# A two-layer attention kernel: steps between the score products reordered, four elementwise pieces moved from VectorE to GpSimd and ScalarE

## The chip, the cores and the metric

The kernel runs on one core of one Trainium2 chip. The metric is the device time of one execution in microseconds (us), lower is better. The engines are called as the profile calls them: PE is TensorE, DVE is VectorE, ACT is ScalarE, POOL is GpSimd, SP is the engine that issues most transfers. Each engine works through its own instructions in order and waits on semaphores.

## The reference

The input x has 128 sequences of 64 tokens of 256 features. Two layers follow one another.

```
L0:  x_mod = rms(x) * (1 + scale_msa) + shift_msa
     q, k, v = split(x_mod @ qkv_w);  q, k = rope(rms(q) * w), rope(rms(k) * w)
     x = x + gate_msa * (softmax(q k^T / 4) v @ proj_w + proj_b)
     h = rms(x) * (1 + scale_mlp) + shift_mlp
     x = x + gate_mlp * ((silu(h @ w1) * (h @ w3)) @ w2)
L1:  self_feat = concat(x, cond or 0 where the row sum is 0) @ W_self^T + b_self
     for d in 0, 1:                        # the adjacency and its transpose
         A = adjacency (64 x 64 x 11), first 20 columns
         aff = q k^T / 4, -9e15 where sum(A) == 0, plus A @ w_bias + b_bias
         output += softmax(aff) @ kv, through Wout, + bout
     result = x + relu(self_feat + output)
```

Shift and scale come per sequence from a condition vector. The float32 products are made of reduced-precision parts: each operand is split into a high part and a low rest (`nh`, `nl` and others).

## The kernel before

Features lie on the partitions, tokens in the free dimension. The 8192 tokens are done in NM = 32 blocks of MT = 256 tokens (4 sequences), so a typical tile is 128x512 (DC = 2 halves of the features by 256 tokens). `ORDER` is a schedule written out by hand: for each engine a list of (a, step, n), run once per iteration m; an entry stands for the step of block m + a. So an iteration works on up to four blocks at once: the second layer of block m, the MLP of block m + 1, the first attention of m + 2, and norm and qkv of m + 3. An iteration is called a period below. Engines meet only through semaphores, called signals here; `wait(engine, signal, m, n)` waits for the n-th count of block m, and `wait_last` for everything of the blocks before m, which protects a buffer. `wait_free` on PE waits until the last readers of a PSUM bank are done.

The steps that matter below, with the lines of the profile:

- End of an iteration. PE makes the MLP's last products (`mlp_down`, L744 is its last part). Its input is a product on DVE, which ACT copies to `gh` (L982), and whose rest POOL makes as `gl` (L1372). DVE adds the second attention to `sf` (`mix1`, L1333), takes an inverse root (`rope_scale`, L1190), and makes the result `out` (L1339): y = max(sf, 0) + x2. SP stores y (L507).
- Start of the next iteration. DVE scales q and k (`rope`, L1196, once for each of two token tiles), then gates the MLP's output (`mlp_down`, L1262), POOL adds the residual x1 (L1420), ACT copies to `nh` (L995), POOL makes the rest `nl` (L1372). PE sums the rows with `ones_r` and multiplies with the self weights (`self`). DVE's `mlp_down` waits for `relu_done` of the block before, because `out` reads x2.
- POOL goes on with `heads` (`kbd`, L1384), adds x_res to x1 (`proj`, L1415) and splits sf (`self_split`, L1372).
- DVE reduces the weighted edges and makes their bias (`edge_masks`, L1284, L1285, L1287). PE makes the scores of the first attention, and DVE takes their maximum and subtracts it (`score_max` L1206, `score` L1211, for two tiles), with `norm1_squares` (L1140), `norm1_mean` (L1145) and `k1` (L1294) in between.
- The norm of the MLP: ACT squares x1, DVE adds the two halves (L1140), PE takes the mean (`norm1_mean`, L580), DVE adds eps, POOL takes the power (L1368), PE spreads the result over the partitions (`norm1_apply`, L587), POOL scales (L1404), DVE multiplies (L1153) and shifts (L1162), ACT copies to `nh` and POOL makes `nl`. The norm of the next block (`norm0_...`, scale L1394) does the same for qkv.

```
            def out(m, n):
                wait(dve, summed1, m, DC)
                wait_last(dve, out_s, m)
                nc.vector.scalar_tensor_tensor(y[:, :, :], sf[:, :, :], 0.0, x2[:, :, :], ALU.max, ALU.add)
            def mlp_down(m, n):
                wait(dve, down_done, m, 1)
                wait_last(dve, relu_done, m)
```

Of the kernel before, what the change touches and what calls it, by code (L numbers as in the profile page):

```python
# [37 lines left out]
DC = D // P  # L38
# [33 lines left out]
LOW_PARTS = {("norm0_shift", 0): (2, 4), ("rope", 1): (4, 7), ("score", 1): (7, 9), ("mix", 1): (9, 12), ("mlp_up", 1): (12, 14)}  # L72
# [13 lines left out]
        (0, "q1", 0), (0, "q1", 1), (0, "q1_low", 0), (1, "norm1_mean", 0), (0, "q1_low", 1), (1, "norm1_apply", 0),  # L86
# [7 lines left out]
        (2, "rope", 0), (2, "rope", 1), (0, "mlp_down", 0), (1, "mixT", 0), (1, "proj", 0), (0, "row_mask", 0),  # L94
        (0, "edge_masks", 0), (2, "score_max", 0), (2, "score", 0), (1, "norm1_squares", 0), (2, "score_max", 1),
# [5 lines left out]
        (3, "rope_scale", 0), (0, "out", 0),  # L101
    ],
    "Activation": [
        (2, "rope_scale", 0), (0, "mlp_split", 2), (1, "mixT", 0), (0, "x2_split", 0),
# [73 lines left out]
def build_program(nc, d):  # L178
    with ExitStack() as ctx:
# [3 lines left out]
        def signal(name, per=1):  # L183
            return Signal(ctx.enter_context(nc.semaphore(name)), per)
# [197 lines left out]
        edge_masked, edge_ready = signal("edge_masked"), signal("edge_ready")  # L382
# [5 lines left out]
        relu_done = signal("relu_done")  # L388
# [40 lines left out]
        def _(sp):  # L429
# [444 lines left out]
        def _(act):  # L874
# [122 lines left out]
            def self_feat(m, n):  # L997
                if isinstance(m, int) and m == 0:
                    act.wait_ge(weight_lo.sem, len(PIECES))
                wait(act, self_ps, m, 1)  # L1000
                wait_last(act, relu_done, m)
# [24 lines left out]

            def score1(m, t):
                wait(act, shifted1, m, t + 1)
                e_v = e1[t][:, :, :, 0:NKV].rearrange("p h a k -> p (h a) k")
                nc.scalar.activation(e_v, e_v, ACT.Exp).then_inc(exps1.sem, 1)  # L1030

            def probs_t1(m, t):
# [10 lines left out]
                "score1": score1, "probsT1": probs_t1, "edges": edges,  # L1043
# [6 lines left out]
        def by_seq(ap):  # L1050
            return ap.rearrange("p c (b s) -> p c b s", s=S)

        @block.vector
        def _(dve):
# [66 lines left out]
            def rotation_tables():  # L1121
                dve.wait_ge(sines.sem, 1)
                half = DH // 2
                for i in range(2):
                    for a in range(2):
                        nc.vector.tensor_tensor(cosw[:, i, a * half:(a + 1) * half], lnw[:, i, a * half:(a + 1) * half],
                                                ang[:, 1, :], ALU.mult)
                        last = nc.vector.scalar_tensor_tensor(sinw[:, i, a * half:(a + 1) * half], ang[:, 0, :],
                                                              (1.0, -1.0)[a], lnw[:, i, a * half:(a + 1) * half],
                                                              ALU.mult, ALU.mult)  # L1130
                last.then_inc(table_step.sem, 1)
                dve.wait_ge(table_step.sem, 9)
                low_parts(*LOW_PARTS["norm0_shift", 0])

            dve.wait_ge(zeros_set.sem, 6)
            dve.wait_ge(biases_set.sem, 2)

            def norm1_squares(m, n):
                wait(dve, squares[1], m, 1)
                nc.vector.tensor_tensor(x1_sq[:, 0, :], x1_sq[:, 0, :], x1_sq[:, 1, :], ALU.add).then_inc(square_sums.sem, 1)  # L1140
# [195 lines left out]
            def out(m, n):  # L1336
                wait(dve, summed1, m, DC)
                wait_last(dve, out_s, m)
                nc.vector.scalar_tensor_tensor(y[:, :, :], sf[:, :, :], 0.0, x2[:, :, :], ALU.max, ALU.add)\  # L1339
                    .then_inc(relu_done.sem, 1)  # L1340

            run_steps(dve, "DVE", {
                "norm1_squares": norm1_squares, "norm1_mean": norm1_mean, "norm1_apply": norm_apply(1), "qkv": qkv, "rope_scale": rope_scale,
                "rope": rope, "score_max": score_max, "score": score, "norm0_apply": norm_apply(0),
                "norm0_shift": norm_shift(0), "norm1_shift": norm_shift(1), "mix": mix, "mixT": mix_t, "proj": proj,
                "mlp_up": mlp_up, "mlp_down": mlp_down, "row_mask": row_mask, "edges": edges,
                "k1": k1, "score1_bias": score1_bias, "score1_max": score1_max, "score1": score1, "soft1_inverse": soft1_inverse,
                "edge_masks": edge_masks, "soft1": soft1, "mix1": mix1, "out": out,
            }, {step: partial(low_parts, *pieces) for step, pieces in LOW_PARTS.items()}
                | {("norm0_shift", 0): rotation_tables, ("rope", 1): cond_split})  # L1350
# [3 lines left out]
        def _(pool):  # L1354
# [83 lines left out]
            def soft1(m, t):  # L1438
# [7 lines left out]
                "x2_split": x2_split, "self_split": self_split, "soft1": soft1, "norm0_scale": norm0_scale, "norm1_scale": norm1_scale, "edges": edges,  # L1446
            })
# [47 lines left out]
```

## Time and profile before

| | before |
|---|---|
| median of 3 runs | 1367.35 us (1363.63 to 1369.65) |
| the profiled execution | 1372.13 us, its span 1370.3 us |
| PE busy | 1296.1 us, 95% |
| DVE busy | 1190.3 us, 87% |
| ACT busy | 861.6 us, 63% |
| POOL busy | 718.7 us, 52% |
| granted PE clock | 0.976 of full speed |
| DMA | 53 GB/s mean |

The span is the time between the first and the last instruction that the profiler saw. The busy times overlap. The kernel repeats one pattern, so one period in the middle can be read in place of the whole: its timeline gives for each engine the start of an instruction, its duration, the line, the tiles, and in brackets how long the engine sat idle before it and who ended the wait.

### The profile page before, as it was taken

To read this page: it belongs to the slowest core of one execution; us is meant where nothing else is said; L and a number is where in the kernel's file an instruction comes from. 1 tells how busy PE (TensorE), PEld (TensorE's weight loads), DVE (VectorE), ACT (ScalarE), POOL (GpSimd) and SP (SyncE) were. 2 spreads that over 40 slices of the span, in tenths; PEclk is the share of its full clock that TensorE was granted. 3 is DMA by queue.
4 is the path that set the end of the run, shared out by engine and by line. 5 is a ranking of instruction groups with operands and counts; after the bars stand their busy time and mean duration, and the time that the engine had idled before them with its cause. 6 is when DMAs were issued, how large, how long until landed. Compare 5 with 4: busy or idle time off the path is not lost. (4 is left out here: it accounts for less than half of the span.)

```text
span 1370.3 us, 50527 instructions
## 1 busy us (share of the span) xinstructions
PE 1296.1 (95%) x19956; PEld 1178.2 (86%) x19956; DVE 1190.3 (87%) x2067; ACT 861.6 (63%) x1722; POOL 718.7 (52%) x676
## 2 busy tenths in 40 slices
PE   5689999999999999999999999999999999999985
PEld 4578888988888898888889888888988898999874
DVE  7569899989889898989999898999999999989763
ACT  5456666667666666666666676666667666666542
POOL 2136555555655555565555456555545655554551
PEclk9689999999999999999999999999999999999996
DMA  6101111101111110111111111111111111111110
GB/s 218 60 24 47 61 60 44 59 31 44 59 59 57 46 59 31 44 59 60 54 50 55 35 44 59 59 52 52 47 44 44 59 59 52 52 39 45 45 40 24
DMA packets 72164, 72.98 MB, mean 53 GB/s; under 512 B 5952, under 2 KB 65728, under 8 KB 72128
## 3 DMA queue, kind: packets, MB, share of 16 engines
q1 hardware_dynamic: 71840, 71.96, 16.2%
q10 hardware_dynamic: 288, 0.52, 0.1%
q8 instruction: 25, 0.41, 0.1%
q14 instruction: 11, 0.09, 0.0%
HBM read 55.42 MB, written 17.04 MB: 53 GB/s over the span
## 5 line engine op out<-in xcount | busy, mean ns | idle before, releaser
L1372 POOL TENSOR_TENSOR gl<-gf,gh 128x512 fp32r<-128x512 f32 x96 | 124.7, 1299 | 222.5 <-ACT gh L982 222.5
L519 PE MATMUL psum<-nh,w_lo 128*128 128x256 f32 x704 | 181.0, 289 | 0.0
L519 PE MATMUL psum<-nh,w_hi 128*128 128x256 f32 x704 | 175.4, 281 | 0.0
L1441 POOL TENSOR_TENSOR e<-e,inv 128x640 f32<-128x640 f32 x64 | 82.2, 1284 | 138.6 <-DVE inv L1328 138.6
L1372 POOL TENSOR_TENSOR nl<-xn,nh 128x512 fp32r<-128x512 f32 x64 | 96.0, 1500 | 91.4 <-ACT nh L920 91.4
L519 PEld LDWEIGHTS psum<-nh,w_lo 128*128 128x128 f32 x704 | 133.3, 189 | 0.3 <-issue 0.2
L519 PEld LDWEIGHTS psum<-nh,w_hi 128*128 128x128 f32 x704 | 133.4, 190 | 0.0
L519 PE MATMUL psum<-nl,w_hi 128*128 128x256 f32 x704 | 114.8, 281 | 0.0
L982 ACT ACTIVATE gh<-gf 128x512 fp32r<-128x512 f32 x96 | 60.3, 628 | 61.3 <-DVE gf L1256 60.6
L519 PEld LDWEIGHTS psum<-nl,w_hi 128*128 128x128 f32 x704 | 97.2, 189 | 0.2 <-POOL nl L1372 0.2
L519 PE MATMUL psum<-qkv_lo,nh 128*128 128x512 f32 (+1 forms) x256 | 88.4, 356 | 8.2 <-ACT nh L920 7.4
L967 ACT ACTIVATE aoh<-psum 128x512 fp32r<-128x512 f32 x32 | 19.1, 598 | 109.5 <-PE psum L679 109.5
L519 PE MATMUL psum<-gh,w_lo 128*128 128x256 f32 x320 | 81.6, 289 | 1.6 <-ACT gh L982 0.8
L519 PE MATMUL psum<-qkv_hi,nh 128*128 128x512 f32 (+1 forms) x256 | 82.2, 343 | 0.0
L670 PEld LDWEIGHTS psum<-vb,pT 128*64 128x64 f32 x2048 | 67.1, 141 | 17.5 <-issue 12.7
L1420 POOL TENSOR_TENSOR x<-x 128x256 f32<-128x256 f32 x64 | 45.7, 735 | 69.2 <-DVE x L1262 69.2
L1384 POOL TENSOR_TENSOR kbd<-qkT,consts 128x512 f32<-128x512 f32 x64 | 66.5, 1060 | 29.3 <-ACT qkT L948 29.3
L1206 DVE TENSOR_REDUCE mx<-psum 128x16 f32<-128x1024 f32 x64 | 77.8, 1215 | 2.3 <-PE psum L635 2.2
L1211 DVE TENSOR_TENSOR e<-psum,mx 128x1024 f32<-128x1024 f32 x64 | 78.1, 1220 | 1.4
L519 PE MATMUL psum<-gh,w_hi 128*128 128x256 f32 x320 | 78.1, 278 | 0.0
L655 PE MATMUL psum<-consts,e 128*128 128x128 f32 x512 | 73.3, 289 | 4.4 <-ACT e L953 4.3
L1256 DVE TENSOR_TENSOR gf<-gf,psum 128x512 f32<-128x512 f32 x96 | 66.0, 688 | 11.4 <-PE psum L519 0.3
(193 smaller groups left out, 4319.1 us busy)
## 6 DMA issues: line engine op xcount, KB each, us to landing
adj<-in_adj SPq DMA_DIRECT2D x32, 440.0 KB, 3.3
x_in<-in_x SPq DMA_DIRECT2D x32, 256.0 KB, 2.7
xn<-in_xT SPq DMA_DIRECT2D x32, 256.0 KB, 3.7
x_res<-in_xT SPq DMA_DIRECT2D x32, 256.0 KB, 3.7
v_rows<-stage SPq DMA_DIRECT2D x32, 256.0 KB, 2.0
vb<-v_rows SPq DMA_DIRECT2D x128, 64.0 KB, 1.9
out_T<-y SPq DMA_DIRECT2D x32, 256.0 KB, 2.1
stage<-in_qkv SPq DMA_DIRECT2D x2, 384.0 KB, 6.2
```

Of the source, the lines that this page charges most:

```text
L519: last = nc.tensor.matmul(out, lhsT, rhs, start=start and i == 0, stop=stop and i == len(terms) - 1)
L655: last = nc.tensor.transpose(pT_out[t][j // 4][:, j % 4, :], e0[t][:, 2 * pair(j):2 * pair(j) + 2, :].rearrange("p h s -> p (h s)"), ident ...
L670: last = nc.tensor.matmul(mix_ps[t][s * S:(s + 1) * S, j, :], pT0[:, j, s * S:(s + 1) * S], vb[:, t, s, j, :], start=True, stop=True, tile ...
L967: nc.scalar.activation(aoh[:, :, :].rearrange("p c t -> p (c t)"), aoT_ps, ACT.Copy).then_inc(mixed_hi.sem, 1)
L982: nc.scalar.activation(gh[:, 2 * n:2 * n + 2, :], gf[:, :, :], ACT.Copy).then_inc(g_hi.sem, 1)
L1206: nc.vector.tensor_reduce(mx0_v, s_v[t], AX.X, ALU.max).then_inc(maxima.sem, 1)
L1211: nc.vector.tensor_tensor(e0_v[t], s_v[t], mx0_v.unsqueeze(3).to_broadcast([P, NG, 4, S]), ALU.subtract).then_inc(shifted_s.sem, 1)
L1256: nc.vector.tensor_tensor(gf[:, :, :], gf[:, :, :], u_ps[n], ALU.mult).then_inc(g_done.sem, 1)
L1372: return nc.gpsimd.tensor_tensor(out, full, hi.bitcast(F32), ALU.subtract)
L1384: nc.gpsimd.tensor_tensor(kbd[:, t, :, :, :, :].rearrange("p c s h k -> p (c s) h k"), qkT[t][:, 1, :, :].rearrange("p c (s k) -> p (c s) ...
L1420: nc.gpsimd.tensor_tensor(x2[:, o, :], x2[:, o, :], x1[:, o, :], ALU.add).then_inc(x2_done.sem, 1)
L1441: nc.gpsimd.tensor_tensor(e_v, e_v, inv1[t][:, :].unsqueeze(2).to_broadcast([P, ND * H, NKV]), ALU.mult)\
```

## The change

Work is moved between engines, and steps within an engine's list.

1. `out`: ACT makes y = relu(sf) (new signal `relu_kept`), and POOL adds x2 to y (`relu_done`), after its `mlp_up` 2 and before its `mlp_down`. DVE's instruction goes. `self` on ACT waits for `relu_kept` in place of `relu_done`. ACT's `rope_scale` and `mlp_split` 2 move from the head of the list to its end, one block further on, so that their place in time order is the same.
2. `norm1_squares` moves from DVE to POOL, behind `self_split`. On PE `norm1_mean` moves ahead of `q1_low` 0; on DVE `k1` moves ahead of `norm1_mean`, and both ahead of the second `score_max`.
3. `norm0_shift` moves from DVE to POOL, ahead of `norm0_apply`.
4. The edges: the reduction (`edge_values`) moves ahead of `proj` on DVE. The sum with the bias becomes two additions on POOL (`edge_sum`, new signal `edge_offset`), between `norm0_scale` and `norm1_apply`. SP's load of the next edges waits for `edge_count` and `edge_float` of the block before, no longer for `edge_masked`.
5. The parts of the weights that were split behind `norm0_shift` in the first block are split behind `norm0_apply`.

```diff
 "PE":
-  (0, "q1", 1), (0, "q1_low", 0), (1, "norm1_mean", 0), (0, "q1_low", 1), (1, "norm1_apply", 0),
+  (0, "q1", 1), (1, "norm1_mean", 0), (0, "q1_low", 0), (0, "q1_low", 1), (1, "norm1_apply", 0),
 "DVE":
-  (1, "mixT", 0), (1, "proj", 0), (0, "row_mask", 0),
-  (0, "edge_masks", 0), (2, "score_max", 0), (2, "score", 0), (1, "norm1_squares", 0), (2, "score_max", 1),
-  (1, "norm1_mean", 0), (0, "k1", 0), (2, "score", 1), (1, "norm1_apply", 0), (1, "norm1_shift", 0),
-  (3, "norm0_apply", 0), (3, "norm0_shift", 0), (0, "score1_bias", 0),
+  (1, "mixT", 0), (0, "edge_values", 0), (1, "proj", 0),
+  (0, "row_mask", 0), (0, "edge_masks", 0), (2, "score_max", 0), (2, "score", 0), (0, "k1", 0),
+  (1, "norm1_mean", 0), (2, "score_max", 1), (2, "score", 1), (1, "norm1_apply", 0), (1, "norm1_shift", 0),
+  (3, "norm0_apply", 0), (0, "score1_bias", 0),
...
-  (3, "rope_scale", 0), (0, "out", 0),
+  (3, "rope_scale", 0),
 "Activation":
-  (2, "rope_scale", 0), (0, "mlp_split", 2), (1, "mixT", 0),
+  (1, "mixT", 0),
...
+  (3, "rope_scale", 0), (1, "mlp_split", 2), (0, "out", 0),
 "Pool":
-  (1, "proj", 0), (0, "self_split", 0), (3, "norm0_mean", 0), (1, "norm1_mean", 0), (1, "norm1_scale", 0),
-  (3, "norm0_scale", 0), (1, "norm1_apply", 0), (3, "norm0_apply", 0), (0, "soft1", 0), (1, "mlp_up", 0),
-  (0, "soft1", 1), (1, "edges", 0), (1, "mlp_up", 1), (1, "mlp_up", 2), (1, "mlp_down", 0), (1, "x2_split", 0),
+  (1, "proj", 0), (0, "self_split", 0), (1, "norm1_squares", 0), (3, "norm0_mean", 0), (1, "norm1_mean", 0), (1, "norm1_scale", 0),
+  (3, "norm0_scale", 0), (0, "edge_sum", 0), (1, "norm1_apply", 0), (3, "norm0_shift", 0), (3, "norm0_apply", 0), (0, "soft1", 0), (1, "mlp_up", 0),
+  (0, "soft1", 1), (1, "edges", 0), (1, "mlp_up", 1), (1, "mlp_up", 2), (0, "out", 0), (1, "mlp_down", 0), (1, "x2_split", 0),
...
-                wait_last(sp, edge_masked, m)
+                wait_last(sp, edge_count, m)
+                wait_last(sp, edge_float, m)
...
+            def out(m, n):                      # ACT
+                wait(act, summed1, m, DC)
+                wait_last(act, out_s, m)
+                nc.scalar.activation(y[:, :, :], sf[:, :, :], ACT.Relu).then_inc(relu_kept.sem, 1)
...
+            def out(m, n):                      # POOL
+                wait(pool, relu_kept, m, 1)
+                nc.gpsimd.tensor_tensor(y[:, :, :], y[:, :, :], x2[:, :, :], ALU.add).then_inc(relu_done.sem, 1)
...
+            def norm1_squares(m, n):
+                wait(pool, squares[1], m, 1)
+                nc.gpsimd.tensor_tensor(x1_sq[:, 0, :], x1_sq[:, 0, :], x1_sq[:, 1, :], ALU.add).then_inc(square_sums.sem, 1)
...
+            def edge_sum(m, n):
+                wait(pool, edge_value, m, 1)
+                nc.gpsimd.tensor_tensor(edge_v[:, :, :], edge_v[:, :, :],
+                                        all_edges(edge_b[:, :]), ALU.add).then_inc(edge_offset.sem, 1)
+                wait(pool, edge_masked, m, 1)
+                wait(pool, edge_offset, m, 1)
+                wait_last(pool, biased1, m)
+                nc.gpsimd.tensor_tensor(edge_bias[:, :, :], edge_v[:, :, :], edge_n[:, :, :], ALU.add).then_inc(edge_ready.sem, 1)
...
+            def norm0_shift(m, n):
+                wait(pool, normed[0], m, 1)
+                nc.gpsimd.tensor_tensor(by_seq(xn[0][:, :, :]), by_seq(xn[0][:, :, :]),
+                                        per_seq(mods[:, SHIFT_A:SHIFT_A + DC, bass.ds(m * MB, MB)]), ALU.add)\
+                    .then_inc(shifted[0].sem, 1)
```

## Rows read from the trace of the kernel before

**Rows 1.** Windows view of one period: busy time and instructions of each engine.

```profile
701.10:741.20 40.10, 39.54 (x625) 35.95 (x624) 36.52 (x64) 26.39 (x54) 22.39 (x21) 1.00 0.16 51
```

**Rows 2.** Timeline of PE: start us, duration us, engine, line, operation, tiles, count.

```profile
703.88 0.27 PE L744 MATMUL psum<-gl,w_hi 64*128 64x256 f32 x1
...
707.06 0.40 PE L519 MATMUL psum<-nh,ones_r 128*128 128x256 f32 x2
...
707.77 0.49 PE L519 MATMUL psum<-nl,ones_r 128*128 128x256 f32 x2
...
713.94 0.64 PE L519 MATMUL psum<-sf_lo,q_hi 128*128 128x256 f32 x4
...
714.42 0.50 PE L580 MATMUL psum<-consts,x_sq 128*128 128x1 f32 x4
...
715.94 0.43 PE L587 MATMUL psum<-consts,rms_inv 128*128 128x128 f32 x2 [0.44 <-POOL rms_inv L1368]
...
717.78 1.50 PE L830 MATMUL psum<-kbd,q1T 32*64 32x40 f32 x128
...
728.47 0.39 PE L519 MATMUL psum<-qkv_lo,nh 128*128 128x512 f32 x1
```

**Rows 3.** Timeline of DVE in the same period.

```profile
701.72 1.53 DVE L1339 SCALAR_TENSOR_TENSOR y<-sf,x 128x512 f32<-128x512 f32 x1
703.17 1.28 DVE L1196 TENSOR_TENSOR qr<-qr,qk_inv 128x512 f32<-128x512 f32 x2
704.38 0.74 DVE L1262 TENSOR_TENSOR x<-psum,mods 128x256 f32<-128x256 f32 x2
...
707.48 0.88 DVE L1237 SCALAR_TENSOR_TENSOR x<-psum,consts,mods 128x256 f32<-128x256 f32 x2 [1.30 <-PE psum L519]
...
708.64 1.05 DVE L1284 TENSOR_REDUCE edge_v<-q1T 128x80 f32<-128x880 f32 x1
...
709.83 1.21 DVE L1287 SCALAR_TENSOR_TENSOR edge_bias<-edge_v,consts,edge_n 128x80 f32<-128x80 f32 x1
...
710.96 1.21 DVE L1206 TENSOR_REDUCE mx<-psum 128x16 f32<-128x1024 f32 x1
...
713.35 0.41 DVE L1140 TENSOR_TENSOR x_sq<-x_sq 128x256 f32<-128x256 f32 x1
...
714.96 0.16 DVE L1145 TENSOR_SCALAR rms_root<-psum 128x2 f32<-128x2 f32 x1
...
716.21 1.21 DVE L1211 TENSOR_TENSOR e<-psum,mx 128x1024 f32<-128x1024 f32 x1
...
719.60 0.69 DVE L1162 TENSOR_TENSOR xn<-xn,mods 128x512 f32<-128x512 f32 x1
```

**Rows 4.** Timeline of POOL in the same period.

```profile
701.41 1.29 POOL L1372 TENSOR_TENSOR gl<-gf,gh 128x512 fp32r<-128x512 f32 x1 [5.62 <-ACT gh L982]
...
704.87 1.42 POOL L1420 TENSOR_TENSOR x<-x 128x256 f32<-128x256 f32 x2 [2.17 <-DVE x L1262]
...
706.26 1.44 POOL L1372 TENSOR_TENSOR nl<-x,nh 128x256 fp32r<-128x256 f32 x2
...
709.67 1.27 POOL L1415 TENSOR_TENSOR x<-x,x_res 128x512 f32<-128x512 f32 x1
...
711.25 1.29 POOL L1372 TENSOR_TENSOR sf_lo<-sf,sf_hi 128x512 fp32r<-128x512 f32 x1 [0.31 <-ACT sf_hi L1009]
...
715.20 0.69 POOL L1368 TENSOR_TENSOR rms_inv<-rms_root,minus_half 128x2 f32<-128x2 f32 x1 [1.57 <-DVE rms_root L1145]
...
716.85 1.05 POOL L1394 TENSOR_TENSOR xn<-xn,mods 128x512 f32<-128x512 f32 x1
719.67 1.76 POOL L1372 TENSOR_TENSOR nl<-xn,nh 128x512 fp32r<-128x512 f32 x1 [1.78 <-ACT nh L920]
```

**Rows 5.** Timeline of ACT in the same period.

```profile
706.33 0.42 ACT L995 ACTIVATE nh<-x 128x256 fp32r<-128x256 f32 x1 [0.27 <-POOL x L1420]
```

**Rows 6.** Instructions that write y: shortest, median and longest in ns.

```profile
L1339 DVE SCALAR_TENSOR_TENSOR y<-sf,x x32: 692/1540/1761, 140.4 to 1367.1; 128x512 f32<-128x512 f32 x32
```

More of the change, by code:

```diff
@@ L71 @@
 HIGH_PARTS = {("norm0_apply", 0): (2, 5), ("heads", 1): (5, 9), ("probsT", 0): (9, 12), ("mlp_split", 0): (12, 14)}
-LOW_PARTS = {("norm0_shift", 0): (2, 4), ("rope", 1): (4, 7), ("score", 1): (7, 9), ("mix", 1): (9, 12), ("mlp_up", 1): (12, 14)}
+LOW_PARTS = {("norm0_apply", 0): (2, 4), ("rope", 1): (4, 7), ("score", 1): (7, 9), ("mix", 1): (9, 12), ("mlp_up", 1): (12, 14)}
 BANK = {
@@ L85 @@
         (2, "heads", 1), (1, "proj", 0), (0, "self", 0), (0, "self_cond", 0), (2, "score", 0), (0, "k1", 0),
-        (0, "q1", 0), (0, "q1", 1), (0, "q1_low", 0), (1, "norm1_mean", 0), (0, "q1_low", 1), (1, "norm1_apply", 0),
+        (0, "q1", 0), (0, "q1", 1), (1, "norm1_mean", 0), (0, "q1_low", 0), (0, "q1_low", 1), (1, "norm1_apply", 0),
         (2, "probsT", 0),
@@ L93 @@
     "DVE": [
-        (2, "rope", 0), (2, "rope", 1), (0, "mlp_down", 0), (1, "mixT", 0), (1, "proj", 0), (0, "row_mask", 0),
-        (0, "edge_masks", 0), (2, "score_max", 0), (2, "score", 0), (1, "norm1_squares", 0), (2, "score_max", 1),
[2 rows of a table removed]
+        (2, "rope", 0), (2, "rope", 1), (0, "mlp_down", 0), (1, "mixT", 0), (0, "edge_values", 0), (1, "proj", 0),
+        (0, "row_mask", 0), (0, "edge_masks", 0), (2, "score_max", 0), (2, "score", 0), (0, "k1", 0),
[2 rows of a table added]
         (0, "score1_bias", 1), (0, "score1", 0), (2, "mix", 0), (0, "score1_max", 1), (0, "soft1", 0),
@@ L387, in build_program @@
         mixed1, summed1 = signal("mixed1", TILES), signal("summed1", DC)
-        relu_done = signal("relu_done")
+        relu_kept, relu_done = signal("relu_kept"), signal("relu_done")
         cond_rows_s = signal("cond_rows_s", 16)
@@ L1000, in self_feat @@
                 wait(act, self_ps, m, 1)
-                wait_last(act, relu_done, m)
+                wait_last(act, relu_kept, m)
                 for o in range(DC):
@@ L1042, in _ @@
                 "mlp_up": mlp_up, "mlp_split": mlp_split, "x2_split": x2_split, "self": self_feat, "self_split": self_split, "q1": q1, "v1": v1,
-                "score1": score1, "probsT1": probs_t1, "edges": edges,
+                "score1": score1, "probsT1": probs_t1, "edges": edges, "out": out,
             }, {("norm0_mean", 0): first_weights, ("rope_scale", 0): gate_and_mlp_mods} | {step: partial(high_parts, *pieces) for step, pieces in HIGH_PARTS.items()})
@@ L1132, in rotation_tables @@
                 dve.wait_ge(table_step.sem, 9)
-                low_parts(*LOW_PARTS["norm0_shift", 0])
+                low_parts(*LOW_PARTS["norm0_apply", 0])
             dve.wait_ge(zeros_set.sem, 6)
             dve.wait_ge(biases_set.sem, 2)
-            def norm1_squares(m, n):
-                wait(dve, squares[1], m, 1)
-                nc.vector.tensor_tensor(x1_sq[:, 0, :], x1_sq[:, 0, :], x1_sq[:, 1, :], ALU.add).then_inc(square_sums.sem, 1)
             def norm1_mean(m, n):
@@ L1277, in edges, with edge_values @@
                 wait(dve, adj_s, m, 16)
+                wait_last(dve, edge_ready, m)
                 nc.vector.tensor_reduce(flat[0], adj[:, :, :, :].rearrange("p t e l -> p (t e) l"), AX.X, ALU.add)\
                     .then_inc(edge_count.sem, 1)
+            def edge_values(m, n):
+                wait(dve, edge_weighted, m, 1)
+                wait_last(dve, edge_ready, m)
+                nc.vector.tensor_reduce(flat[1], adw, AX.X, ALU.add).then_inc(edge_value.sem, 1)
             def edge_masks(m, n):
-                wait(dve, edge_weighted, m, 1)
                 wait(dve, edge_count, m, 1)
-                nc.vector.tensor_reduce(flat[1], adw, AX.X, ALU.add).then_inc(edge_value.sem, 1)
                 nc.vector.tensor_scalar(flat[0], flat[0], 0.0, NEG, ALU.is_le, ALU.mult).then_inc(edge_masked.sem, 1)
-                wait(dve, edge_masked, m, 1)
-                nc.vector.scalar_tensor_tensor(flat[2], flat[1], edge_b[:, :], flat[0], ALU.add, ALU.add)\
-                    .then_inc(edge_ready.sem, 1)
             def k1(m, n):
@@ L1334, in mix1 @@
                                                    ALU.add, ALU.add).then_inc(summed1.sem, 1)
[L1336 to L1340, printed above, removed]
             run_steps(dve, "DVE", {
-                "norm1_squares": norm1_squares, "norm1_mean": norm1_mean, "norm1_apply": norm_apply(1), "qkv": qkv, "rope_scale": rope_scale,
+                "norm1_mean": norm1_mean, "norm1_apply": norm_apply(1), "qkv": qkv, "rope_scale": rope_scale,
                 "rope": rope, "score_max": score_max, "score": score, "norm0_apply": norm_apply(0),
-                "norm0_shift": norm_shift(0), "norm1_shift": norm_shift(1), "mix": mix, "mixT": mix_t, "proj": proj,
+                "norm1_shift": norm_shift(1), "mix": mix, "mixT": mix_t, "proj": proj,
                 "mlp_up": mlp_up, "mlp_down": mlp_down, "row_mask": row_mask, "edges": edges,
                 "k1": k1, "score1_bias": score1_bias, "score1_max": score1_max, "score1": score1, "soft1_inverse": soft1_inverse,
-                "edge_masks": edge_masks, "soft1": soft1, "mix1": mix1, "out": out,
+                "edge_masks": edge_masks, "edge_values": edge_values, "soft1": soft1, "mix1": mix1,
             }, {step: partial(low_parts, *pieces) for step, pieces in LOW_PARTS.items()}
-                | {("norm0_shift", 0): rotation_tables, ("rope", 1): cond_split})
+                | {("norm0_apply", 0): rotation_tables, ("rope", 1): cond_split})
         @block.gpsimd
@@ L1446, in _ @@
                 "x2_split": x2_split, "self_split": self_split, "soft1": soft1, "norm0_scale": norm0_scale, "norm1_scale": norm1_scale, "edges": edges,
+                "norm1_squares": norm1_squares, "edge_sum": edge_sum, "norm0_shift": norm0_shift, "out": out,
             })
```

6 lines of the change are left out of this document (4 added, 2 removed), and 2 rows, old and new, of the table ORDER.

## The prediction

> **What bounds the kernel.** I read the windows view of one period first, then the timelines of PE, DVE, POOL and ACT over that period, and last the durations of the instruction that goes. A period is 40.10 us. PE is busy 39.54 of it, DVE 36.52, ACT 26.39, POOL 22.39 [rows 1]. The reader is to see that PE is the tightest engine, with 0.56 us a period that the profile calls idle, and that DVE, though busy nine tenths, is second. So work taken off DVE pays only where PE waits for DVE, and work put on POOL costs where PE waits for POOL. Two places are like that.
>
> Place A is the turn of the period. The MLP's last product starts on PE at 703.88 and ends at 704.15 [rows 2]. DVE then gates it at 704.38, just as `rope` ends (703.17 + 1.28 = 704.45) [rows 3]; POOL adds it at 704.87 and makes its rest until 707.70 (706.26 + 1.44) [rows 4]; ACT's second copy ends at 706.75 [rows 5]. PE starts the row sums at 707.06, 0.31 us behind that copy, and their low part at 707.77, 0.07 us behind POOL [rows 2, 4]. So a delay of the gate reaches PE whole. POOL does not rest from 704.87 to 710.94 (709.67 + 1.27) [rows 4], hence neither can it catch up there.
>
> Place B is the MLP's norm. PE takes the mean at 714.42, DVE adds eps at 714.96, POOL's power ends at 715.89 and PE goes on at 715.94 after the wait in brackets, 0.44 us [rows 2, 3, 4]. That wait is most of the idle PE time.
>
> **The change at place A: POOL adds x2.** DVE's y instruction took 1.53 us, from 701.72 to 703.25 [rows 3]. Its shortest is 692 ns, its median 1540 [rows 6]. POOL's `gl` ran from 701.41 to 702.70 [rows 4], so y ended 0.55 us behind it: an instruction with both inputs in SBUF stood still until POOL was through. The same is seen at L1287, a small 128x80 sum that took 1.21 us and ended at 711.04, 0.10 us behind POOL's addition at 710.94 [rows 3, 4]. So the two exclude each other for a whole instruction. That sets the sum. The next DVE instruction, `rope`, also has both inputs in SBUF, and takes y's slot: it will stand still from 701.72 to 702.70. Relu on ACT is ready in time: a 128x256 ACT instruction takes 0.42 [rows 5], so 128x512 takes at most 0.84, and from 701.72, when the sum for `out` is surely done, it ends by 702.56. Then three pieces share the time from 702.70, one after another: rope 0, rope 1 and POOL's addition. Before, it was y's rest 0.55 and 1.28 less an overlap of 0.08, which brought the end of rope to 704.45. After, it is 0.55 for the first rope, 1.27 for the addition (L1415 has its form and size [rows 4]) and about 0.60 for the second rope: 705.12. In each of the three possible orders the sum is the same, and the gate needs both rope and the addition (`relu_done`). It starts 0.07 before the end, as before: 705.10 if rounded up, against 704.38. The loss is **0.72 us** a period. Behind the gate on DVE wait the low part of `mixT` and `proj`'s gate, which has 1.30 us of idle time before it [rows 3]; on POOL all of 704.87 to 710.94. Behind ACT's Relu and its wait is the first copy of the next period, whose input comes from PE after 704.15, so that wait costs nothing.
>
> [...]
>
> The bounds of this loss: 0 if rope does not contend; 0.46 if the 0.31 of slack before the row sums, less 0.05 for PE's reaction (715.89 to 715.94), can be used and the low part does not bind; 0.72 + 0.31 = 1.03 if the heads' transposes wait for the second rope as well. I take 0.72, since the low part had 0.07 to spare only.
>
> No row shows a Relu. If it brought a table load, the add could start later than 702.70, but both ropes would pass first, and the end stays near 705.1: nothing is added to the sum.
>
> [...]
>
> **The change at place B.** `norm1_squares` on DVE was 0.41 us [rows 3]. POOL is free behind `sf_lo` at 712.54 (711.25 + 1.29) and needs 0.71 for a 128x256 addition (1.42 for two [rows 4]), so it is done at 713.25. PE takes the mean in place of the four low products at 713.94 [rows 2], and DVE may add eps 0.54 later (714.96 - 714.42), at 714.48. DVE has by then `k1`: the first maximum and subtraction still end at 713.35 (slot of L1140), and k1 with the eps instruction takes 716.21 - 714.96 = 1.25 us [rows 3]. So the root is out at about 714.68, POOL's power runs 714.76 to 715.45, and PE goes on at 715.50. Before it was 715.94: a gain of **0.44 us**. The same low products are still done before it, by about 715.3. The second subtraction starts 0.33 earlier (L1140's share without overlap) and ends at 716.21 - 0.33 + 1.21 = 717.09; PE's second-layer scores, at 717.78 before, can start at 717.34. So that gain holds. Bounds: 0 if POOL's queue is late, 0.56 at most, all of PE's idle time.
>
> **What is hidden.** `norm0_shift`: 0.69 on DVE [rows 3], about 1.05 on POOL (L1394, the same broadcast form [rows 4]). It comes behind `nl` of the other norm (719.67 + 1.76) and its rest is made by about 724; PE's qkv reads it at 728.47 [rows 2]. Without those 4 us of cover it would cost 1.05 - 0.69 = 0.36 a period. `edge_sum`: the trace shows no such POOL instruction; it lies between nothing and 0.71 each (128x256), so at most 1.42 together, in the 1.78 us that POOL idled before 719.67 [rows 4]. I take 0.37 each, between the ends since 128x80 is nearer to the small one. The 1.05 us reduction L1284 moves into the 1.30 us of idle before L1237 [rows 3]; L1287 goes. But the next DVE instruction, the first maximum, then waits for PE's scores, so of the 2.26 us that leave this place at most 0.1 shows, which I leave out. SP: the store waits about 1.3 to 1.9 us longer, and behind it the condition rows and three loads. They are read 4 us or more later. The next edges are loaded earlier and read late in the period. The moved split of the weights concerns the first block alone: nothing.
>
> **Sum.** DVE loses 3.8 us of work a period, its waits for POOL counted in (1.53, 1.21, 0.69, 0.41), POOL gains about 3.8, yet PE's path gets 0.72 - 0.44 = +0.28 us. Of 32 blocks some 30 turn with all four blocks at work: +8.4 us. At the very end, relu and the addition stand bare: 0.62 (estimated from 0.42 for half the size) + 1.27 - 0.69 = +1.2. Together +9.6. The profiled execution took 1372.13 (span 1370.3), and would take 1381.7. It lies 4.8 above the median of the runs, 1367.35, so for that I say 1377.0, +0.7%.
>
> **Rivals.** *The addition is hidden*: POOL idles 2.17 us before 704.87 [rows 4], more than 1.27. If rope does not have to take turns with it, the gate can start 0.1 behind PE's end, at 704.25, and the gain of place B stays: -0.57 x 30 + 1.2 = -16, 1351.5. For it: rope's second input is only 64 columns, broadcast. Against it: L1287's were small too and it waited. It decides if rope's two instructions end before POOL's addition or run beside it at 0.68 each. *Loss alone*: POOL's longer queue eats the gain of place B: 0.72 x 30 + 1.2 = +22.8, 1390. Against it: POOL has 0.69 us to spare before 713.94. *DVE was the bound*: 3.8 us a period, -114; the 39.54 of PE exclude more than 0.56 x 30 = -17, so it gives 1351 with the first. *Slack hides a part*: 0.46 - 0.44, about 0 a period, 1369, no change to be measured.
>
> **Numbers.** The forecast 0.50, hidden addition or DVE as the bound together 0.27, slack 0.13, loss alone 0.10. A measurement of this kernel can tell about 0.5%, 6.8 us. Of the forecast's 0.50 a fifth stays within that. So slower 0.40 + 0.10 = 0.50, same 0.10 + 0.13 = 0.23, faster 0.27. The range takes in both outer cases: 1350 to 1391. The likeliest case's own range is 1370 to 1386 (a loss between 0.5 and 1.0 a period less the gain).
>
> **What would show it.** In the profile after: a period of 40.4 us; the first or the second rope instruction of each pair near 1.5 us or more in place of 0.68; the gate at least 0.6 us later behind PE's last MLP product than now (0.50 from start to start); a new PE wait before the low row sums, for POOL's `nl`; the wait before PE's `norm1_apply` nearly gone. I am wrong if rope stays at 0.68, or if the gate follows PE's end at once.

## The result and the profile after

The changed kernel takes 1374.19 us (median of 19 runs, 1370.12 to 1376.6), the kernel before 1368.48 us (median of 19 runs, 1363.48 to 1373.65). The ratio on record is 1.0033, with a 95% interval of 1.0022 to 1.0044. By it the change makes the kernel 4.5 us slower (3.0 to 6.0); the two medians differ by 5.7 us. Either is less than the 0.5% that the forecast counts as a change. I had forecast +9.6 us.

The windows view of one period of the changed kernel, from one gate (`mlp_down` on DVE, now L1265) to the next; the columns are those of [rows 1].

```profile
703.20:743.39 40.19, 39.94 (x624) 36.05 (x623) 34.87 (x61) 26.92 (x55) 26.32 (x26) 1.00 0.15 51
```

The period is 40.19 us in place of 40.10. DVE is busy 34.87 in place of 36.52, POOL 26.32 in place of 22.39. PE is busy 39.94 in place of 39.54, though it does the same products: some are shown longer, as the two high row sums below, 0.50 in place of 0.40 [rows 2]. So "busy" of PE is no measure of what can be gained here: an experiment below makes the same products in a whole period of 39.71 us, less than the 39.94 that PE is called busy here.

The turn of the period. DVE's timeline of the changed kernel, which answers to rows of [rows 3]:

```profile
700.16 3.12 DVE L1199 TENSOR_TENSOR qr<-qr,qk_inv 128x512 f32<-128x512 f32 x2
703.20 0.74 DVE L1265 TENSOR_TENSOR x<-psum,mods 128x256 f32<-128x256 f32 x2
...
709.71 1.23 DVE L1209 TENSOR_REDUCE mx<-psum 128x16 f32<-128x1024 f32 x1 [2.07 <-PE psum L637]
...
713.30 0.16 DVE L1148 TENSOR_SCALAR rms_root<-psum 128x2 f32<-128x2 f32 x1
...
714.63 1.23 DVE L1214 TENSOR_TENSOR e<-psum,mx 128x1024 f32<-128x1024 f32 x1
```

ACT's Relu in the same period:

```profile
699.70 0.64 ACT L1032 ACTIVATE y<-sf 128x512 f32<-128x512 f32 x1
```

POOL's timeline, which answers to [rows 4]:

```profile
699.75 1.30 POOL L1370 TENSOR_TENSOR gl<-gf,gh 128x512 fp32r<-128x512 f32 x1 [5.64 <-ACT gh L984]
701.00 1.73 POOL L1422 TENSOR_TENSOR y<-y,x 128x512 f32<-128x512 f32 x1
703.69 1.43 POOL L1418 TENSOR_TENSOR x<-x 128x256 f32<-128x256 f32 x2 [0.96 <-DVE x L1265]
705.09 1.42 POOL L1370 TENSOR_TENSOR nl<-x,nh 128x256 fp32r<-128x256 f32 x2
...
713.53 0.69 POOL L1366 TENSOR_TENSOR rms_inv<-rms_root,minus_half 128x2 f32<-128x2 f32 x1 [0.55 <-DVE rms_root L1148]
...
716.19 0.32 POOL L1439 TENSOR_TENSOR edge_v<-edge_v,consts 128x80 f32<-128x80 f32 x1
716.74 0.76 POOL L1444 TENSOR_TENSOR edge_bias<-edge_v,edge_n 128x80 f32<-128x80 f32 x1 [0.23 <-POOL edge_v L1439]
...
719.31 1.04 POOL L1448 TENSOR_TENSOR xn<-xn,mods 128x512 f32<-128x512 f32 x1
```

The reader is to see the three pieces in turn. The two rope instructions take 3.12 us in place of 1.28. A timeline over a narrower window parts them:

```profile
700.16 1.43 DVE L1199 TENSOR_TENSOR qr<-qr,qk_inv 128x512 f32<-128x512 f32 x1
...
701.51 1.76 DVE L1199 TENSOR_TENSOR qr<-qr,qk_inv 128x512 f32<-128x512 f32 x1
```

The first stands still behind `gl` (until 701.05) and ends at 701.59. The addition stands still behind the first rope (it takes 1.73; at the end of the run, alone, 1.26) and ends at 702.73. The second rope stands still behind the addition and ends at 703.28 (700.16 + 3.12). From `gl`'s end to the gate it is 703.20 - 701.05 = 2.15 us, and was 704.38 - 702.70 = 1.68 [rows 3, 4]: 0.47 us later.

PE's timeline, which answers to [rows 2]:

```profile
702.22 0.27 PE L746 MATMUL psum<-gl,w_hi 64*128 64x256 f32 x1
...
705.62 0.50 PE L521 MATMUL psum<-nh,ones_r 128*128 128x256 f32 x2
706.56 0.51 PE L521 MATMUL psum<-nl,ones_r 128*128 128x256 f32 x2
...
708.37 1.21 PE L637 MATMUL psum<-kbd,qkT 32*64 32x128 f32 x64
...
712.76 0.50 PE L582 MATMUL psum<-consts,x_sq 128*128 128x1 f32 x4
...
714.28 0.43 PE L589 MATMUL psum<-consts,rms_inv 128*128 128x128 f32 x2
...
716.22 1.50 PE L832 MATMUL psum<-kbd,q1T 32*64 32x40 f32 x128
```

Counted from the start of `gl`, the low row sums stand at 706.56 - 699.75 = 6.81 us, and stood at 707.77 - 701.41 = 6.36: +0.45, and +0.47 one product on. The second layer's scores (L832) stand at 16.47 and stood at 16.37: +0.10. So PE loses 0.47 at place A and gets 0.38 back at place B (0.39 by the periods of the experiments), and the period grows by 0.09 us. The wait in brackets before L589 is gone.

Over 29 periods that is 2.6 us. At the end of the run, ACT's Relu starts at 1367.08 and the addition ends at 1367.78 + 1.26 = 1369.04; before, y ended at 1367.1 + 0.69 = 1367.8 [rows 6]: +1.2. Together 3.8 us, inside the measured 3.0 to 6.0.

### The profile page after: what moved, and what is told of

It reads as the page before. It is cut to its first block and busy times, and to the rows that moved or that the text cites. A ratio compares the mean times of both kernels' runs of the same rounds, so it can differ in the third digit from the quotient of the medians.

```text
span 1371.6 us, 50740 instructions
## 1 busy us (share of the span) xinstructions
PE 1304.2 (95%) x19956; PEld 1176.5 (86%) x19956; DVE 1141.2 (83%) x1939; ACT 878.0 (64%) x1754; POOL 843.4 (61%) x836
## 5 line engine op out<-in xcount | busy, mean ns | idle before, releaser
L1370 POOL TENSOR_TENSOR nl<-xn,nh 128x512 fp32r<-128x512 f32 x64 | 83.1, 1298 | 48.2 <-ACT nh L922 48.2
L1199 DVE TENSOR_TENSOR qr<-qr,qk_inv 128x512 f32<-128x512 f32 x64 | 95.3, 1528 | 1.4
L1042 ACT ACTIVATE pT<-psum 128x512 f32<-128x512 f32 x64 | 38.3, 598 | 59.1 <-PE psum L849 58.4
L849 PE MATMUL psum<-consts,e 128*128 128x128 f32 x512 | 69.9, 280 | 5.9 <-POOL e L1465 5.9
```

The source lines that it names most:

```text
L849: last = nc.tensor.transpose(pT1_out[t][j // 4][:, j % 4, :], e1[t][:, 2 * pair(j):2 * pair(j) + 2, :, :].rearrange("p h a k -> p (h a k)" ...
L1042: nc.scalar.activation(pT1[:, 0:4, :], pT1_out[t][0], ACT.Copy).then_inc(pT1_a.sem, 1)
L1199: nc.vector.tensor_tensor(q_v, q_v, qk_inv[:, t, :].unsqueeze(2).to_broadcast([P, 2 * H, DH]), ALU.mult)\
L1370: return nc.gpsimd.tensor_tensor(out, full, hi.bitcast(F32), ALU.subtract)
```

## The experiments

All times are against the kernel before on the same chip. The experiments ran on three chips, so ratios and periods are compared, not times. The period is read from gate to gate.

**Place A alone.** The kernel before, with `out` moved as in the change and nothing else.

```diff
 # the kernel before
-  "DVE": (0, "out", 0)   y = max(sf, 0) + x2
+  "Activation": (0, "out", 0)   y = relu(sf)
+  "Pool": (1, "mlp_up", 2), (0, "out", 0), (1, "mlp_down", 0)   y = y + x2
```

> The kernel before, with out alone moved (Relu on ACT, the addition of x2 on POOL). Theory: at the turn of the period the two rope instructions and the addition take turns, and PE gets 0.48 us a period later to the low row sums, as in the changed kernel (from gl's end to the gate 2.15 us in place of 1.68). With nothing to give it back the period is 40.10 + 0.48 = 40.58 us, and the time about 14 + 1.5 us longer than before, +1.1%. Rival one, the loss comes from the longer POOL queue around the norm (squares, edge sum, shift): this kernel is then within 0.2% of before. Rival two, ACT's and POOL's hops are hidden by PE's slack: the same, no change.

It took 1382.85 us, ratio 1.0105 (1.0085 to 1.0126). The timeline of DVE in this kernel, two gates:

```profile
706.74 0.74 DVE L1268 TENSOR_TENSOR x<-psum,mods 128x256 f32<-128x256 f32 x2
...
747.35 0.74 DVE L1268 TENSOR_TENSOR x<-psum,mods 128x256 f32<-128x256 f32 x2
```

The period is 40.61 us, +0.51. Both rivals fall: the moved result alone costs 14 us (12 to 17).

**Place A undone.** The changed kernel, with `out` back on DVE.

```diff
 # the changed kernel
-  "Activation": (0, "out", 0)   "Pool": (0, "out", 0)
+  "DVE": (3, "rope_scale", 0), (0, "out", 0)   y = max(sf, 0) + x2
```

> The changed kernel, with out back on DVE as one instruction. Theory: the turn costs nothing again and the gain at the norm stays: 40.19 - 0.48 = 39.71 us a period, about 0.39 x 29 = 11 us under before, -0.8%. Rival: the loss is in the other moves; then it stays at 40.1 to 40.2 us a period, +0.1 to +0.3% against before.

It took 1358.66 us, ratio 0.9924 (0.9903 to 0.9944).

```profile
738.11 0.74 DVE L1260 TENSOR_TENSOR x<-psum,mods 128x256 f32<-128x256 f32 x2
...
777.82 0.74 DVE L1260 TENSOR_TENSOR x<-psum,mods 128x256 f32<-128x256 f32 x2
```

The period is 39.71 us, to the hundredth as expected. So the change holds a gain of 0.39 us a period and spends 0.48 of it on the moved result.

**The size of the addition.** Two kernels change it and leave Relu and the order as they are. In the first, POOL adds two columns only, so x2 is missing in the rest of the result.

```diff
 # the changed kernel
-  nc.gpsimd.tensor_tensor(y[:, :, :], y[:, :, :], x2[:, :, :], ALU.add).then_inc(relu_done.sem, 1)
+  nc.gpsimd.tensor_tensor(y[:, 0, 0:2], y[:, 0, 0:2], x2[:, 0, 0:2], ALU.add).then_inc(relu_done.sem, 1)
```

> The changed kernel with POOL's addition cut to two columns of one half; the rest of x2 is not added to the result. Relu on ACT, the signals and their order stay. Theory one, the time of the shared turn (rope, addition, rope) makes the loss: gate again 2.85 to 2.97 us behind gl's start, 39.6 to 39.75 us a period, -0.8% against before. Theory two, the hops through ACT and POOL (Relu, two signals, POOL's own start) make it: it stays within 0.15 of 40.19 us.

It took 1358.16 us, ratio 0.9925 (0.9899 to 0.9950). POOL's timeline and DVE's gates:

```profile
731.70 0.64 POOL L1422 TENSOR_TENSOR y<-y,x 128x2 f32<-128x2 f32 x1
```

```profile
733.36 0.76 DVE L1265 TENSOR_TENSOR x<-psum,mods 128x256 f32<-128x256 f32 x2 [0.47 <-PE psum L746]
...
773.06 0.76 DVE L1265 TENSOR_TENSOR x<-psum,mods 128x256 f32<-128x256 f32 x2 [0.47 <-PE psum L746]
```

The period is 39.70 us. The gate now waits for PE, and starts 2.92 us behind `gl`'s start (730.44), as before the change (2.97). So the hops through ACT and POOL cost nothing, and the time in the shared turn does. The small addition took 0.64 us, where its shortest in this run is 0.19: it too stood behind the first rope.

In the second kernel the addition is made twice, with one more signal between the two, so the result has x2 twice.

```diff
 # the changed kernel
+  nc.gpsimd.tensor_tensor(y[:, :, :], y[:, :, :], x2[:, :, :], ALU.add).then_inc(once.sem, 1)
+  wait(pool, once, m, 1)
   nc.gpsimd.tensor_tensor(y[:, :, :], y[:, :, :], x2[:, :, :], ALU.add).then_inc(relu_done.sem, 1)
```

> The changed kernel with the addition of x2 done twice by POOL; the result has x2 twice. Theory: another 1.27 us in the chain to the gate, plus some 0.1 us for the signal between, all of it on PE's path: 41.5 us a period, +38 us against the changed kernel. If only the semaphore order mattered and POOL's idle time could take the addition, it would stay under 40.6.

It took 1419.24 us, ratio 1.0375 (1.0348 to 1.0403).

```profile
720.76 1.73 POOL L1422 TENSOR_TENSOR y<-y,x 128x512 f32<-128x512 f32 x1
722.56 1.60 POOL L1424 TENSOR_TENSOR y<-y,x 128x512 f32<-128x512 f32 x1
```

```profile
724.40 0.76 DVE L1265 TENSOR_TENSOR x<-psum,mods 128x256 f32<-128x256 f32 x2 [1.37 <-POOL y L1424]
...
766.03 0.76 DVE L1265 TENSOR_TENSOR x<-psum,mods 128x256 f32<-128x256 f32 x2 [1.37 <-POOL y L1424]
```

The period is 41.63 us, +1.44. The second rope slipped in between the two additions: the second addition took 1.60 in place of 1.26, though it had started only 0.07 behind the first one's end. The gate starts 4.90 us behind the start of `gl` (719.50), and started 3.45 behind it in the changed kernel (703.20 - 699.75). So the whole delay of the gate reaches PE, to 0.01 us.

**The gate between the ropes.**

```diff
 # the changed kernel
 "DVE":
-  (2, "rope", 0), (2, "rope", 1), (0, "mlp_down", 0),
+  (2, "rope", 0), (0, "mlp_down", 0), (2, "rope", 1),
 "PE":
-  (2, "heads", 1), (1, "proj", 0), (0, "self", 0),
+  (1, "proj", 0), (2, "heads", 1), (0, "self", 0),
```

> The changed kernel, with DVE's gate (mlp_down 0) between the two rope instructions and PE's heads 1 behind proj. Theory: rope and the addition exclude each other, but the gate reads PSUM and only waits for the addition's end; it starts some 0.1 us behind the addition, 1.75 us behind gl's end in place of 2.15. PE then has no transposes to fill its wait for aoh, so some of it is given back: the low row sums come about 0.2 us earlier, 40.0 us a period, about 0.0% against before. Rival, the gate is late because of what comes before the addition (Relu, gl): then it starts where it started, and the period is 40.2 us or more.

It took 1385.84 us, ratio 1.0126 (1.0104 to 1.0148): a miss. DVE's timeline, then POOL's:

```profile
712.59 1.43 DVE L1199 TENSOR_TENSOR qr<-qr,qk_inv 128x512 f32<-128x512 f32 x1
715.40 0.76 DVE L1265 TENSOR_TENSOR x<-psum,mods 128x256 f32<-128x256 f32 x2 [1.38 <-POOL y L1422]
716.07 1.10 DVE L1199 TENSOR_TENSOR qr<-qr,qk_inv 128x512 f32<-128x512 f32 x1
717.10 0.68 DVE L1229 TENSOR_TENSOR aol<-psum,aoh 128x512 fp32r<-128x512 f32 x1
```

```profile
713.43 1.73 POOL L1422 TENSOR_TENSOR y<-y,x 128x512 f32<-128x512 f32 x1
715.91 1.87 POOL L1418 TENSOR_TENSOR x<-x 128x256 f32<-128x256 f32 x2 [0.74 <-DVE x L1265]
```

The gate did start earlier, 1.93 us behind `gl`'s end in place of 2.15, but 0.24 behind the addition where I expected 0.1. Then the second rope met POOL's next piece, the addition of x1: rope took 1.10 in place of 0.68, POOL 1.87 in place of 1.43, and both `aol` (PE waited 0.3 us for it) and `nl` came later. PE also had no transposes to fill its wait for `aoh` (0.41 us). The period is 40.64 us. The turn was moved, not removed. The number fits the rival (40.2 or more), but its reason does not: the gate did not start where it had started.

**Place B, the order of q1.**

```diff
 # the changed kernel, "PE"
-  (0, "q1", 0), (0, "q1", 1), (1, "norm1_mean", 0), (0, "q1_low", 0), (0, "q1_low", 1),
+  (0, "q1", 0), (0, "q1_low", 0), (0, "q1", 1), (1, "norm1_mean", 0), (0, "q1_low", 1),
```

> The changed kernel, with PE's order q1 0, q1_low 0, q1 1, norm1_mean, q1_low 1, so that ACT can copy q1's first half sooner. Theory: in the changed kernel PE waits 0.2 us before norm0_apply for ACT's copy out of the same PSUM bank, because both q1_low stand behind norm1_mean; here the wait goes and the period is 40.0 us, -0.2 us x 29 = -6 us against the changed kernel, so -0.1% against before. Rival: that wait is the issue of the many semaphore waits on PE; then nothing changes, 40.19 us, +0.3%.

It took 1390.35 us, ratio 1.0151 (1.0129 to 1.0173), the period is 40.67 us: a miss, by a slip of mine. With `q1_low` 0 ahead, the mean stands 0.47 us later on PE behind the first attention's scores (L637 at 718.02, L582 at 722.88; 708.37 and 712.76 in the changed kernel). DVE's next steps all wait behind the eps instruction. DVE's timeline, then PE's:

```profile
721.75 1.25 DVE L1298 SCALAR_TENSOR_TENSOR kbd<-psum,consts 128x160 f32<-128x160 f32 x4
723.41 0.16 DVE L1148 TENSOR_SCALAR rms_root<-psum 128x2 f32<-128x2 f32 x1 [0.41 <-PE psum L582]
723.50 1.23 DVE L1209 TENSOR_REDUCE mx<-psum 128x16 f32<-128x1024 f32 x1
724.75 1.23 DVE L1214 TENSOR_TENSOR e<-psum,mx 128x1024 f32<-128x1024 f32 x1
```

```profile
724.40 0.43 PE L589 MATMUL psum<-consts,rms_inv 128*128 128x128 f32 x2 [0.44 <-POOL rms_inv L1366]
...
726.34 0.89 PE L832 MATMUL psum<-kbd,q1T 32*64 32x40 f32 x68 [0.42 <-DVE e L1214]
```

The slip is worth having. It splits the two things that end at place B: PE's last wait is not for the norm but for `e`, the second subtraction, and L832 follows its end (725.98) by 0.36 us. In the kernel's text PE's `score1` waits for `shifted_s`, this subtraction's signal, because both layers' scores use the same PSUM bank. The distance is the same before (717.42 to 717.78 [rows 2, 3]) and after (715.86 to 716.22), so already before the change it was `e` that PE's second-layer scores waited for.

**Place B, squares or norm.** On top of the kernel with `out` back, the squares go back to DVE, and PE's order stays.

```diff
 # the changed kernel with out back on DVE
-  "Pool": (0, "self_split", 0), (1, "norm1_squares", 0), (3, "norm0_mean", 0),
+  "Pool": (0, "self_split", 0), (3, "norm0_mean", 0),
-  "DVE": (2, "score_max", 0), (2, "score", 0), (0, "k1", 0),
+  "DVE": (2, "score_max", 0), (2, "score", 0), (1, "norm1_squares", 0), (0, "k1", 0),
```

> The kernel of the run before with out back on DVE (39.72 us a period), and norm1_squares back on DVE as well, behind the first subtraction and ahead of k1; PE's mean stays early. Theory one, the chain at place B is DVE's own queue: from the scores two maxima, two subtractions, k1 and the eps instruction stand one behind another up to PE's second-layer scores, so the 0.33 us of the squares come back whole: 40.05 us a period, -0.1% against before. Theory two, as predicted, the chain is the norm's (mean, power, PE's wait for it): DVE's squares would be done by the time PE takes the mean, so the period stays at 39.7, -0.8%.

It took 1365.74 us, ratio 0.9978 (0.9961 to 0.9995); the gates stand at 702.34 and 742.34, a period of 40.00 us. DVE's timeline, then PE's:

```profile
748.86 1.22 DVE L1208 TENSOR_REDUCE mx<-psum 128x16 f32<-128x1024 f32 x1 [2.07 <-PE psum L637]
750.11 1.22 DVE L1213 TENSOR_TENSOR e<-psum,mx 128x1024 f32<-128x1024 f32 x1
751.25 0.41 DVE L1142 TENSOR_TENSOR x_sq<-x_sq 128x256 f32<-128x256 f32 x1
751.59 1.25 DVE L1297 SCALAR_TENSOR_TENSOR kbd<-psum,consts 128x160 f32<-128x160 f32 x4
752.76 0.15 DVE L1147 TENSOR_SCALAR rms_root<-psum 128x2 f32<-128x2 f32 x1
752.82 1.22 DVE L1208 TENSOR_REDUCE mx<-psum 128x16 f32<-128x1024 f32 x1
754.07 1.22 DVE L1213 TENSOR_TENSOR e<-psum,mx 128x1024 f32<-128x1024 f32 x1
```

```profile
755.65 1.50 PE L832 MATMUL psum<-kbd,q1T 32*64 32x40 f32 x128 [0.40 <-DVE e L1213]
```

Of the 0.39 us, 0.29 are gone with the squares on DVE, though the mean was ready in time: PE began it at 751.91, and DVE added eps 0.85 us later, where 0.54 is enough (712.76 to 713.30 in the changed kernel). So at place B DVE's own queue is what pays, from the first maximum to the end of the second subtraction. It takes 717.42 - 710.96 = 6.46 us before, 715.86 - 709.71 = 6.15 in the changed kernel and 755.29 - 748.86 = 6.43 here.

Most of the last tenth comes from in front of that queue. PE's scores of the first attention in the kernel before:

```profile
709.56 1.21 PE L635 MATMUL psum<-kbd,qkT 32*64 32x128 f32 x64
```

The first maximum started 710.96 - 709.56 = 1.40 us behind them, right behind the sum of the edges, and starts 709.71 - 708.37 = 1.34 behind them in the changed kernel, and as much here. But the queue is not alone. In the changed kernel DVE adds eps 0.54 us behind PE's mean, as before (714.42 to 714.96 [rows 2, 3]), just as `k1` ends (712.11 + 1.25 = 713.36): mean and queue are tied there. That is why the 0.47 us by which the mean came later in the run above cost a full 0.48 a period. The earlier mean is needed for the gain, and so are the squares off DVE.

**What the other moved pieces are worth.** `norm0_shift` and the sum of the edges go back to DVE too; the squares alone stay on POOL.

```diff
 # the changed kernel with out back on DVE
-  "Pool": (3, "norm0_scale", 0), (0, "edge_sum", 0), (1, "norm1_apply", 0), (3, "norm0_shift", 0), (3, "norm0_apply", 0),
+  "Pool": (3, "norm0_scale", 0), (1, "norm1_apply", 0), (3, "norm0_apply", 0),
-  "DVE": (3, "norm0_apply", 0), (0, "score1_bias", 0)
+  "DVE": (3, "norm0_apply", 0), (3, "norm0_shift", 0), (0, "score1_bias", 0)   # the edges' sum is in edge_masks again
```

> The kernel with out back on DVE (39.72 us a period), and norm0_shift and the sum of the edges back on DVE too, so that of the four moved pieces only norm1_squares is on POOL, beside the new orders. Theory: both were hidden on POOL and have room on DVE (idle 2.08 us before the scores, nothing waits early for the shift), so nothing changes: 39.70 to 39.80 us a period, -0.75% against before. Rival: DVE's load counts, 1.9 us more of it costs up to 0.4 us a period, 40.1.

It took 1357.95 us, ratio 0.9922 (0.9898 to 0.9946).

```profile
735.16 0.74 DVE L1260 TENSOR_TENSOR x<-psum,mods 128x256 f32<-128x256 f32 x2
...
774.92 0.74 DVE L1260 TENSOR_TENSOR x<-psum,mods 128x256 f32<-128x256 f32 x2
```

From these two gates the period is 39.76 us; over the run they are 39.71 to 39.76, as with the pieces on POOL. Moving these two is worth nothing, either way.

**The bank of q1, mended.** On that last kernel, an order that keeps the mean early and still frees the bank sooner.

```diff
 # the kernel of the run above, "PE"
-  (0, "q1", 0), (0, "q1", 1), (1, "norm1_mean", 0), (0, "q1_low", 0), (0, "q1_low", 1),
+  (0, "q1", 0), (0, "q1_low", 0), (1, "norm1_mean", 0), (0, "q1", 1), (0, "q1_low", 1),
```

> The kernel with all but norm1_squares back on DVE and the new orders (39.72 us a period), with PE's order q1 0, q1_low 0, norm1_mean, q1 1, q1_low 1: the mean stays early, and ACT can copy q1's first half sooner, which frees the PSUM bank that PE's norm0_apply writes. Theory: that wait (0.2 us on PE) ends at the same time as DVE's second subtraction allows the second-layer scores, 0.37 us behind it; with the wait gone the subtraction still sets the start, so 39.7 us a period, -0.75% against before, and no more. Rival: the bank is what binds; then 39.5 us a period, -1.3%.

It took 1355.33 us, ratio 0.9905 (0.9885 to 0.9925). PE's timeline:

```profile
747.81 0.38 PE L574 MATMUL psum<-consts,rms_inv 128*128 128x128 f32 x2
748.59 1.50 PE L832 MATMUL psum<-kbd,q1T 32*64 32x40 f32 x128 [0.40 <-DVE e L1209]
```

The wait for the bank is gone: L574 starts 747.81 - 735.57 = 12.24 us behind the gate, and 747.64 - 735.16 = 12.48 in the run above. The wait for `e` has taken its place; DVE's gates stand at 735.57 and 775.27, and 39.7 us is still the period. The mean too is earlier: PE begins it at 744.65, 3.91 us behind the first attention's scores (740.74), where it was 712.76 - 708.37 = 4.39 in the changed kernel, and DVE adds eps only 1.04 us behind it. That is worth nothing either: with both out of the way DVE's queue alone sets the start. Its interval overlaps those of the other kernels with a period of 39.7 us, so I don't call it faster than they are. It beats both kernels of the case, the changed one by some 1.3% (0.9905 / 1.0033).

## Why the prediction was right, and where its sizes were off

**The turn (place A): the mechanism was right, the size too large.** The three pieces in turn, the gate last, POOL's chain and PE's low row sums behind it: all of it is in the trace, and shown by the runs with a small and a double addition. The term was 0.72 and measured 0.47 to 0.51 us. Of the 0.25 too much, 0.05 is a slip in the adding: from `gl`'s end the three pieces give 0.55 + 1.27 + 0.60 = 2.42, and less the 0.07 by which the gate starts early 2.35, not the 2.40 that the prediction calls "rounded up". So its own terms give a loss of 0.67. The trace has 2.15. The other 0.20 is that the sum gave each piece its full duration behind the last. The addition took 702.73 - 701.59 = 1.14 of the turn, not 1.27, the second rope 0.55, not 0.60, and the gate started 0.08 before rope's end, not 0.07. I had read that for y (0.55 in place of 0.69) and not carried it to the addition.

**Place B: the size nearly right, the reason half wrong.** The forecast was 0.44 and it measured 0.38. But I named the norm's wait (mean, power, spread) as the thing that ends last, since the profile put a wait in brackets there, and mentioned DVE's second subtraction only as one that would be ready. PE's `norm1_apply` stood 715.94 - 701.41 = 14.53 us behind the start of `gl` and stands 714.28 - 699.75 = 14.53 behind it now, in spite of the 0.47 lost in front: the norm itself gained 0.47, a little more than forecast. The scores behind it gained 0.38 only, since the next wait, for `e`, stood right behind the one that vanished. With the measured 0.36 us behind the subtraction, the prediction's own end of it (717.09) gives 717.45 for the scores, a gain of 0.33 and not 0.44. The rest, some 0.06, is the earlier first maximum, which the prediction put at "at most 0.1" and left out. That the forecast was so near is in part luck: the same edits shortened both chains.

**The bound "all of PE's idle time", 0.56 us, was no bound.** The busy time of PE grew by 0.40 us for the same products, to more than a whole period of the kernel with `out` back on DVE. It did no harm here, since the gain stayed under it; no run here has a period below the 39.54 us that PE was called busy before.

**The hidden parts** were hidden: 0.32 and 0.76 us for the sums of the edges (bounds 0 to 0.71 each; the second, over its bound, started at 716.74, while DVE's shift L1165, which reads two SBUF operands, ran until 717.29), 1.04 for the shift, and no PE wait behind either. Relu made no table load: it took 0.64 us, and its start at 699.70 follows `gh` (699.06 + 0.62) at once. ACT has 66 ACT_TABLE_LOAD of 1.28 us in the profile of either kernel, at the same steps, and none at Relu's line.

**The signs.** Of those that the prediction named, the blocked ropes came (1.43 and 1.76 us; near 1.5 or more was named for one of the two) and the wait before `norm1_apply` went. The gate starts 703.20 - 702.22 = 0.98 us behind PE's last MLP product, 0.48 more than the 0.50 before, where at least 0.6 more was named. The period is 40.19 where 40.4 was named, and the profile puts no PE wait in brackets before the low row sums. DVE's busy time fell by 1.65 us, not by 3.8, mostly because the two ropes now take 1.84 us longer.

**The sum.** 0.28 us a period was forecast, 0.09 came, because a quarter of a microsecond too much was put on the loss (and 0.06 too much on the gain). Two terms of near equal size and opposite sign leave a small difference. Its sign was right, but the error of the loss alone, 0.25, is nearly as large as the forecast difference, so the sign owes something to luck. The end of the run cost the 1.2 us that were forecast. "Slower by over 0.5%", to which I gave 0.50, did not come true; what came is "same" at 0.5%, to which I gave 0.23. The measured time lies between the forecast and the slack rival (1369, +0.1%), though slack had no part in it: the low row sums came later by the whole delay of the gate.

What stays open: the first gate of the run lies anywhere from 97.8 to 103.8 us in these profiles, without a pattern by kernel; I did not look for the cause. The single profiled executions of the two kernels can't be compared over the whole run for this reason.

## What to carry to other kernels

Before work is moved from DVE to POOL, look at what stands beside it in time. Where it had both inputs in SBUF, and so had the DVE instruction next to it, the two took turns in all eleven profiles here, down to an addition of 128x2 (POOL's power, below, is the one exception seen), and the move that looked like 1.53 us off DVE put a piece of 1.73 us in the same line. Ask of each move which queue, from which event to which, gets shorter; of four pieces moved here one (0.33 us of squares) made the gain, together with the new orders around it, two made nothing, and one cost more than the gain. And where a wait is named in the profile, look at the next one behind it before counting the gain.

## What the runs showed of the hardware

- At the turn of the period a DVE and a POOL instruction that both read two SBUF operands took turns for whole instructions, in both directions: rope behind `gl` (1.43 us in place of 0.68), the addition behind rope (1.73 in place of 1.26), and even a 128x2 addition took 0.64 us in place of 0.19. The turn passed back and forth: with two additions only 0.07 us apart, DVE's rope got in between.
- What did not take turns in the kernel before: DVE's subtraction L1211, which reads PSUM and one SBUF tile, took 1.21 us from 716.21 and POOL's L1394 beside it 1.05 from 716.85 [rows 3, 4]; DVE's reduction L1284, with one SBUF input, took 1.05 us from 708.64 beside `kbd` (L1384, 707.67 to 709.70); and the squares L1140 took 0.41 us from 713.35 beside POOL's power on 128x2 (L1362, 712.92 to 713.62). With one input it could go the other way too: in the last experiment DVE's L1288, a 128x80 instruction with one SBUF input, took 1.10 us from 739.84, until 0.06 behind `kbd` (738.85 + 2.03), and its shortest there is 0.18.
- In the period shown some 0.12 to 0.14 us of the blocked POOL addition and of the blocked DVE product overlapped the piece in front: they added 1.14 and 0.55 us to the turn, where they took 1.26 and 0.68 to 0.69 alone. Which part of the instruction that is, no run here shows.
- PE's first product after DVE's second subtraction started 0.36 us behind its end before the change, after it and in the experiments whose lines are shown, and as the median over the blocks in all eleven profiles; PE followed POOL's power by 0.05 us [rows 2, 4]. Six waits stand before the first step and one before the second; I did not try them one by one, so the cause of the difference stays open.
